# A decoder block on one core: one fill and one LayerNorm schedule moved, the first two FFNs started four slots earlier, and five waits changed

## The reference

```
x = x + selfattn(layernorm(x))        # q, k, v, o projections with biases, causal softmax
x = x + crossattn(layernorm(x), ctx)  # q = layernorm(x), k = v = ctx, causal, no projections
n = layernorm(x)
out = x + relu(n @ W_up.T) @ W_down.T + rw * (n @ W_expert)   # rw: sum of softmax over the top 2
```

## Time and profile before

| what | us |
|---|---|
| median of 3 executions | 713.16 (711.97 to 713.25) |
| the profiled execution | 711.97 |
| its span | 710.0 |
| VectorE busy | 494.6 |
| ScalarE busy | 501.4 |
| GpSimd busy | 256.9 |

### The profile page before, as it was taken

How to read it: one execution, slowest core, us unless ns; L and a number is a source line. 1 busy time by engine, 2 the same in 40 slices (tenths; PEclk the granted TensorE clock), 3 DMA queues, 4 the chain that set the end, 5 groups by cost and what they waited for, 6 DMA issues and landing times.

```text
span 710.0 us, 13884 instructions
## 1 busy us (share of the span) xinstructions
PE 674.7 (95%) x4488; PEld 523.8 (74%) x4488; DVE 494.6 (70%) x1730; ACT 501.4 (71%) x1450; POOL 256.9 (36%) x391
## 2 busy tenths in 40 slices
PE   7998999999999999999889987999989999899998
PEld 6777777777787777777666755777768777677786
DVE  6568766766766776776878788767887669664632
ACT  5678877777876778787899887776588667874110
POOL 4745644333555335742564415333112102000100
PEclk9999999999999999999999999999999999999999
DMA  9763533336423573445946584633463443510101
GB/s 313 186 155 75 141 70 90 82 94 185 116 61 90 124 212 84 102 105 146 275 122 168 153 236 121 166 95 97 96 183 89 111 101 87 163 38 1 59 1 59
DMA packets 52327, 86.12 MB, mean 121 GB/s; under 512 B 8609, under 2 KB 16801, under 8 KB 52257
## 3 DMA queue, kind: packets, MB, share of 16 engines
q1 hardware_dynamic: 52256, 85.25, 46.1%
HBM read 27.55 MB, written 7.34 MB: 49 GB/s over the span
## 4 chain that ended last, share of the span: by engine, by line
PE 80%; DVE 7%; ACT 6%; issue 2%; DMA 2%; POOL 2%; SPq 1%; POOLq 0%; ACTq 0%; DVEq 0%
PE t L480 16%; PE m L519 14%; PE m L520 14%; PE m L521 14%; PE pv L513 9%; PE s L466 8%; DVE probs L682 3%; ACT probs L910 3%; ACT prob L919 1%; PE m L585 1%; DVE prob L692 1%; DMA stack<-stage 1%; POOL probs L1023 1%; PE m L480 1%; PE m L534 1%
## 5 line engine op out<-in xcount | busy, mean ns | idle before, releaser
L682 DVE CUSTOM_DVE_ANT_0 probs<-s,mask 128x128 f32<-128x128 f32 (+3 forms) x512 | 246.6, 483 | 130.7 <-PE s L466 129.0
L910 ACT ACTIVATE probs<-probs,negmax 128x128 f32<-128x128 f32 (+3 forms) x512 | 284.5, 559 | 46.1 <-DVE negmax L682 45.2
L480 PE MATMUL t<-ident,probs 128*128 128x128 f32 x1140 | 203.5, 277 | 11.4 <-ACT prob L919 6.5
L466 PE MATMUL s<-stack 96*128 96x128 f32 (+3 forms) x512 | 197.8, 394 | 5.5 <-DVE negmax L682 2.8
L1023 POOL TENSOR_SCALAR probs<-probs,rsum 128x128 f32<-128x128 f32 (+3 forms) x256 | 133.4, 539 | 176.9 <-DVE rsum L696 176.6
L919 ACT ACTIVATE prob<-t 128x384 f32<-128x384 f32 (+1 forms) x231 | 124.7, 540 | 97.7 <-PE t L480 96.7
L480 PEld LDWEIGHTS t<-ident,probs 128*128 128x128 f32 x1140 | 144.7, 141 | 60.6 <-ACT prob L919 10.5
L466 PEld LDWEIGHTS s<-stack 96*128 96x128 f32 x512 | 97.9, 191 | 18.7 <-DVE negmax L682 4.1
L910 ACT ACTIVATION_READ_ACCUMULATOR probs<-probs,negmax 128x1 f32 x512 | 98.9, 193 | 0.0
L692 DVE COPY prob<-t 128x256 f32<-128x256 f32 (+1 forms) x218 | 77.1, 354 | 30.9 <-PE t L480 29.9
L519 PE MATMUL m<-xT_hi,w_lo 128*128 128x512 f32 x192 | 78.3, 408 | 1.2 <-DVE xT_lo L750 1.2
(11 more groups left out here) (144 smaller groups left out, 946.2 us busy)
## 6 DMA issues: line engine op xcount, KB each, us to landing
stack<-stage SPq DMA_DIRECT2D x384, 128.0 KB, 2.3
xt<-in_x SPq DMA_DIRECT2D x16, 256.0 KB, 4.7
xres<-in_x SPq DMA_DIRECT2D x4, 1024.0 KB, 6.1
kraw<-in_ctxT SPq DMA_DIRECT2D x16, 256.0 KB, 3.0
cv<-in_ctx SPq DMA_DIRECT2D x16, 256.0 KB, 3.1
x<-xres SPq DMA_DIRECT2D x3, 1024.0 KB, 5.5
res<-x SPq DMA_DIRECT2D x8, 256.0 KB, 6.4
out<-res SPq DMA_DIRECT2D x2, 1024.0 KB, 4.8
```

The costliest lines, as they stand in the source:

```text
L466: nc.tensor.matmul(score_tile(P, i), stack[0:RS, P % 2, h, 0, chunk(qb)], stack[0:RS, P % 2, h, 1, 0:N], start=True, stop=True).then_inc(s ...
L480: mm = nc.tensor.transpose(dst[:, chunk(qb - kb)], probs[:, (2 * P + h) % 3, OFF[qb] + PART * kb:OFF[qb] + PART * kb + PART], ident[:, :])
L682: nc.vector.tensor_tensor_reduce(probs[:, (2 * P + h) % 3, OFF[qb]:OFF[qb + 1]], score_tile(P, i), mask[:, T - N:T], -SCALE, BIG, ALU.add, ...
L910: nc.scalar.activation(tile, tile, ACT.Exp, bias=negmax[:, P % 2, h, qb:qb + 1], scale=-1.0, accum_out=total).then_inc(p_exp, 1)
```

## The change

- FEED: the FFNs start at slots 340, 404, 472 and 536; the first two 4 slots sooner. The gap of 4 slots without fills after the second becomes one of 8.
- stats_slots: norm 5 has its four statistics in slots 272, 272, 273, 273 instead of 256, 256, 272, 272; norm 6 in 344, 345, 348, 349 instead of 339 to 342 (with that, ln_scale(6) goes from step 42 to step 43).
- plan: L(b,3) one slot sooner (slot 0 of its step, not 1), O(b,3) of batches 0 and 1 too; FL at distances 1, 3, 5, 7 instead of 1, 2, 4, 5.
- turn: in cross attention, one wait for all four exponentials of the head stands ahead of the first transposes, instead of one wait ahead of each.
- FG: part c multiplies lo and hi of chunk c, instead of hi of all chunks in parts 0 and 1 and lo in 2 and 3.
- GpSimd no longer waits for VectorE's norms 5 to 7 and the four FFN norms ahead of the key split.

```diff
--- before.py
+++ after.py
@@ -74,7 +74,7 @@
 WARM = 24
 
 
-FEED = tuple(PAIRS * (PAIRS * (f + B + 1) + 2) + PAIRS for f in range(B))
+FEED = tuple(PAIRS * (PAIRS * (f + B + 1) + 2) + 4 + 4 * (f // 2) for f in range(B))
 
 
 def own(G):
@@ -104,8 +104,8 @@
         z -= 2 * PAIRS if j == B else 0
         return [z - 8, z - 7, z, z + 1]
     if j == B + 2:
-        return [z + 19, z + 20, z + 21, z + 22]
-    return [z, z, z + 16, z + 16] if j == B + 1 else [z, z, z + 1, z + 1]
+        return [z + 24, z + 25, z + 28, z + 29]
+    return [z + 16, z + 16, z + 17, z + 17] if j == B + 1 else [z, z, z + 1, z + 1]
 
 
 def norm_slots(j):
@@ -148,7 +148,7 @@
             if b:
                 put(("V", b, t), PAIRS * b - 3 + t, 4, 4)
                 if t:
-                    put(("L", b, t), PAIRS * b - 5, 4 + t + 2 * (t // 3), 1)
+                    put(("L", b, t), PAIRS * b - 5, 4 + t + t // 3, 1)
             else:
                 put(("V", b, t), t - 2, 4, 4)
             if b == B - 1:
@@ -156,13 +156,13 @@
             elif b == B - 2:
                 put(("O", b, t), (25, 28, 29, 29)[t], 4 * (t // 3), 4)
             else:
-                put(("O", b, t), PAIRS * (b + 1) + 1 + t, (4, 4, 0, 1)[t], 4)
+                put(("O", b, t), PAIRS * (b + 1) + 1 + t, 4 if t < 2 else 0, 4)
     for f in range(B):
         u = feed_start(f)
         put(("FG", f), 0, u + GATE_AT, 4, 3)
         for m in range(KC):
             if f < B - 1:
-                put(("FL", f, m), 0, u + 1 + m + m // 2, 1, 1)
+                put(("FL", f, m), 0, u + 1 + 2 * m, 1, 1)
             put(("FU", f, m), 0, u + UP_AT + 4 * m, 4)
             put(("FE", f, m), 0, u + EXP_AT + 4 * m, 4)
             put(("FD", f, m), 0, u + DOWN_AT + 4 * m, 4)
@@ -469,14 +469,14 @@
             def turn(P, i):
 
                 h, kb = divmod(i, NT)
+                if kb == 0 and not own(P // 2):
+                    pe.wait_ge(p_exp, PAIRS * P + NT * (h + 1))
                 if TURN_BEFORE[P, i] is not None:
                     pe.wait_ge(*emptied(TURN_BEFORE[P, i]))
                 dst = turned_tile(P, i)
                 for qb in range(kb, NT):
                     if kb == 0 and own(P // 2):
                         pe.wait_ge(p_done, PAIRS * own_rank(P) + NT * h + qb + 1)
-                    elif kb == 0:
-                        pe.wait_ge(p_exp, PAIRS * P + NT * h + qb + 1)
                     mm = nc.tensor.transpose(dst[:, chunk(qb - kb)],
                                              probs[:, (2 * P + h) % 3, OFF[qb] + PART * kb:OFF[qb] + PART * kb + PART],
                                              ident[:, :])
@@ -577,13 +577,11 @@
                         pe.wait_ge(f_ln, NT * (n + 1))
                     turn_x(dst, f_xln, m).then_inc(fl_mm, 1)
                 elif kind == "FG":
+                    pe.wait_ge(fl_lo, KC * n + c + 1)
                     if n == 0 and c == 0:
                         pe.wait_ge(g_lo_done, 1)
-                    done, x_part = (fl_hi, xT_hi) if c < KC // 2 else (fl_lo, xT_lo)
-                    for k in (2 * c % KC, 2 * c % KC + 1):
-                        pe.wait_ge(done, KC * n + k + 1)
-                        mm = nc.tensor.matmul(dst, g_both[:, k, :], x_part[:, k, :], start=(c == 0 and k == 0),
-                                              stop=(c == KC - 1 and k == KC - 1))
+                    nc.tensor.matmul(dst, g_both[:, c, :], xT_lo[:, c, :], start=(c == 0), stop=False)
+                    mm = nc.tensor.matmul(dst, g_both[:, c, :], xT_hi[:, c, :], start=False, stop=(c == KC - 1))
                     if c == KC - 1:
                         mm.then_inc(gate_mm, 1)
                 elif kind == "FU":
@@ -1107,12 +1105,6 @@
                 if own(s // 2):
                     for qb in range(NT):
                         scaled(s, 1, qb)
-                for j in range(B + 1, 2 * B):
-                    if s == norm_slots(j)[-1] // PAIRS:
-                        pool.wait_ge(ln_done, NT * (j + 1))
-                for f in range(B):
-                    if s == f_norm_slots(f)[-1] // PAIRS:
-                        pool.wait_ge(f_ln, NT * (f + 1))
                 if s % 2 == 0 and other(s // 2 + 2):
                     keys(s // 2 + 2)
                 if own((s + 1) // 2):
```

## The result

| | before | after |
|---|---|---|
| median (range, executions) | 712.70 (711.97 to 713.25, 4) | 722.98 (721.55 to 724.09, 4) |
| the profiled execution | 711.97 | 721.66 |
| its span | 710.0 | 719.6 |
| mean granted clock | 0.995 | 0.990 |

The changed kernel is slower: ratio 1.0144, interval 1.0119 to 1.0168. The forecast was 715.0, its range ended at 717.9. A second measurement of the same changed kernel, among the experiments, gave 1.0086 (1.0066 to 1.0106). Both lie on the slower side, and neither is as small as the forecast's 1.0027 (1.9 of 712). So the direction was right and the size was not.

What follows compares the result with a forecast made beforehand. TensorE, busy 674.7 of 710 us, was taken as the bound, with VectorE or ScalarE bounding stretches around the FFNs. Terms summed to +1.9 on 711.97, giving 713.9, stated as a median of 715.0; range 711.5 to 717.9.

Steps and rivals of the forecast that it cites:

- point 1: L3 and O3 moved to slot 0 make TensorE wait ahead of the values: +4.0 us over three batches.
- 4: First FFN's earlier start and norm 6's moved statistics use VectorE's idle time in slots 336 to 351: -1.9 us.
- point 6: Gap after the second FFN, 12 to 16 slots without matmul parts, slots 464 to 484: -1.3 us.
- 3: Without GpSimd's waits the key split runs beside step 42's four FFN norms: +0.9 us on VectorE, counted in 4.
- point 5: Gap after the first FFN, now slots 400 to 411, priced by ScalarE's work, and the gate's turn leaving later: -0.6 us.
- point 2: Norm 5's statistics leave slot 256, two stand in 273, and GpSimd's next scaling starts later: +0.2 us.
- 4, step 44: In step 44 the gate's 8 matmuls are replaced by 12 of FU, less a wait that goes: +0.7 us.
- the hole: A 0.5 us hole in ScalarE's work in the present gap, added once for both FFN gaps: +0.5 us.
- 7: Last FFN's new gate order leaves one more matmul after the last xT_lo, +0.2 us; merged exponentials wait, +0.1.
- rival C: Clearly slower: opening gains nothing and low clock enters the 16 slots without matmuls; +5.5 us, 718.7, chance 0.08.

Runs made afterwards that it cites:

- e11_after_stats: Changed kernel with the statistics of norms 5 and 6 back in their old slots: 723.46 us, 1.0120 against the kernel before.
- a2_after: Changed kernel run again unchanged, the table's second profile of after: 719.80 us, 1.0086 against the kernel before.
- e2_wait: Kernel before without GpSimd's waits for VectorE's norms, nothing else changed: 714.86 us, 0.9994.
- e8b_after_wait: Changed kernel with GpSimd's waits for the norms put back, timed in a later job beside the changed kernel: 718.19 us, 1.0072 against the kernel before.
- e1_lo: Kernel before with only L(b,3) and O(b,3) moved one slot sooner: 719.89 us, 1.0081.
- e10_after_fl: Changed kernel with FL back at the old distances 1, 2, 4, 5: 717.17 us, 1.0042 against the kernel before.
- e3: Kernel before with the change's FEED and FL distances, nothing else: 717.40 us, 1.0036.
- e5: Kernel before with the change's FEED alone, FL at its old distances: 715.03 us, 1.0017.
- c1: Kernel before with all four FFNs 4 slots sooner, FL at its old distances: 715.58 us, 1.0019.
- c2_all4_stats: Kernel before with all four FFNs 4 slots sooner and norm 6's statistics in the changed kernel's slots: 711.72 us, 0.9962.
- b2_before: Kernel before run again unchanged, the table's second profile of before: 714.13 us, span 711.9.
- e4_gate_turn: Kernel before with the new order of FG and the merged wait for the exponentials: 713.35 us, 0.9989.
- e8: Changed kernel with GpSimd's waits for the norms put back, first timing: 718.72 us, 1.0062 against the kernel before.
- e9: Changed kernel with L(b,3) and O(b,3) back in their old slots: 714.94 us, 1.0020 against the kernel before.

## Why the prediction was wrong

The sum was +1.9 and the profiled executions differ by 9.6; without the start, the second pair of profiles differs by 6.9. The sign held because point 1 held, the one large loss that I had. The size failed because the gains of points 4 and 6 didn't come: I forecast -1.9 and -1.3, and they measured -0.6 and +0.9. Of the 5.0 us between 1.9 and 6.9, point 6 is 2.2, points 3 and 4 are 1.3, point 1 is 0.8 and point 5 is 0.7. The terms, in the order of the prediction:

| point | predicted | after against before | after, again against before, again |
|---|---|---|---|
| 1, L3 and O3 | +4.0 | +4.7 | +4.8 |
| 2, norm 5 | +0.2 | +0.3 | +0.3 |
| 3 and 4, slots 328 to 352 | -1.9 | +1.1 | -0.6 |
| 4, step 44 | +0.7 | +0.7 | +0.7 |
| 5, first gap, with the hole's +0.5 | -0.1 | +0.6 | +0.6 |
| 6, second gap | -1.3 | +0.9 | +0.9 |
| 7, tail and merged wait | +0.3 | +0.25 | +0.25 |
| the start | 0 | +1.1 | -0.9 |

**1 was right in its mechanism, and in size for two of three batches.** O3 waited 0.72 and L3 0.44 where I said 0.8 and 0.7, the steps of b = 2 and 3 grew by 1.67 and 1.64 (predicted 1.65). For b = 1 I had 0.7 and the step grew by 1.37. Slot 32 is 1.38 longer (L3's wait of 0.86 and its 0.6) and slot 33 0.44 shorter, as worked, but then slots 34 to 36 are 0.41 longer: there I had taken 0.2 off for a wait that would shorten, and instead the turn of a tile into an m bank came to wait for the evacuation of L3:

```profile
76.17 0.33 PE L480 MATMUL m<-ident,probs 128*128 128x128 f32 x1 [0.55 <-DVE xT_lo L766]
```

That the turns use the m banks too was in the description of the kernel, and I had followed only the fills.

**2 and the step 44 term of 4** came out in size. For point 2, e11_after_stats takes 0.2 of its 0.3 back, and kernels with the old plan of this place differ among themselves by 0.1 (87.24 to 87.35).

**3 failed in its price.** I read 0.79 for a norm beside a GpSimd operation as the price of any overlap, 0.25 each. That norm had only the end of the other engine's operation before it, and even so it waited for that end. This is the subtraction beside it, in the profile of before:

```profile
285.44 1.29 POOL L1058 TENSOR_TENSOR stage<-kraw,stage 128x512 fp32r<-128x512 f32 x1
```

It ends at 286.73 and the norm of the earlier trace rows at 287.02, 0.29 later. The rows after show the same with more left to wait: the first subtraction ends at 435.68 and the pair of norms at 435.97. In the profiles of all runs there are 103 of these 128x512 operations that took longer than 0.57 us, and each of them ended 0.28 to 0.29 us after the end of a GpSimd operation, however long that still had to run. So the price of an overlap is the time that GpSimd's operation has left, less about 0.26 (an estimate: 0.54 alone less 0.28), and not a fixed 0.25. The two pairs took 2.01 and 1.98 us instead of 1.00 and 0.91, so +2.1 and not +0.9. a2_after has 2.01 and 1.78, e2_wait 2.02 for its first pair. The Trainium skill ("SBUF — State Buffer", Who interferes with whom) calls the shared port pair an exclusive lock, and I wrote that the trace did not agree. Read to the end, both traces agree with it. By the rule I had 2.7 for the four norms, by my reading at most 1.0; 2.1 came. I also gave the key splits beside the norms of the later FFNs nothing. In step 50 of the changed kernel, VectorE and GpSimd:

```profile
520.84 1.28 POOL L1056 TENSOR_TENSOR stage<-kraw,stage 128x512 fp32r<-128x512 f32 x1
```
```profile
521.07 1.79 DVE L743 TENSOR_SCALAR f_xln<-res,f_mv,f_rstd 128x512 f32<-128x512 f32 x2
```

That pair takes 1.00 in e8b_after_wait. It is 0.5 of point 5 (400 to 424 at 29.93 there against 30.45).

**4 failed on the basis of comparison and on the first part of the gate.** "I give 2.8 of it back", the idle time of VectorE. Against a profile of before that has the usual low stretch, 0.6 came back (from slot 336 on 0.5, and 0.2 against e1_lo with 22.56). The runs name three things. The norms took 1.2 more than I gave them (2.1 instead of 0.9), and the waits put back recover 0.5 of the stretch from 336 on. The distances of FL cost 1.1 (e10_after_fl 28.90 against 30.00), and from 336 on 2.0 (20.30 against 22.32): the third part one slot later and the fourth two let the gate's first part wait 2.18 for an xT_lo, which is 0.44 in e10, and e10 has one low stretch here where a2_after has two. That holds with the statistics moved; with the statistics in their old slots I can't see a cost of the distances here (24.23 in e3, 24.52 and 22.94 in e5 and c1 without them). I wrote that this wait "is inside this", which was an assertion, without a sum behind it. And before's profile was 1.6 below its second one in this stretch, so part of what I subtracted from was luck; the mean clock of 0.92 in the earlier trace rows is one low stretch in 21.5 us where the other profile has two. The statistics are the part that works: -3.7 from c1_all4 to c2_all4_stats and +3.0 in e11_after_stats when taken back. And the early start with them alone does open the stretch as I had thought: c2 takes 19.53 from 336 on, 3.3 less than b2_before. The distances (2.0) and the norms beside GpSimd (0.5) used most of it up.

**5 failed by norms that had no term, not at the gate's turn.** Slots 416 to 419 take 7.41 (predicted 7.4), and 420 to 423 take 0.46 less (predicted 0.45). But slots 400 to 415 take 18.07 where my sum of ScalarE's prices had 16.85, or 17.35 with the hole's 0.5. With GpSimd's waits put back they take 17.55. So 0.5 is the norm pair that I had given nothing, and the sum with its hole was right within 0.2. (The terms that I name for it, 3.08, 7.05 and 6.57, add up to 16.70; the 16.85 has 0.15 more that the text doesn't explain.)

The same 16 slots by stretch, first of the changed kernel with the four slots behind them, then of e8b_after_wait. The new plan's gap answers to the last four stretches of the earlier trace rows:

```profile
518.60:536.70 18.10, 15.07 (x122) 11.65 (x121) 16.39 (x56) 15.09 (x45) 6.27 (x7) 1.00 0.64 176
536.70:544.10 7.40, 7.40 (x63) 5.06 (x62) 4.91 (x19) 4.79 (x15) 0.00 (x0) 1.00 0.61 142
```
```profile
517.50:535.00 17.50, 14.97 (x121) 11.59 (x120) 15.82 (x56) 15.01 (x45) 4.43 (x5) 1.00 0.65 182
```

ScalarE has the same 15.0 to 15.1 us of work in both; VectorE has 0.6 more and GpSimd is busier in the first, and the stretch is 0.5 longer.

**6 failed by the clock.** The 16 slots took 16.08 us to the score of 480, where I said 15.9, and the gate's wait came, 1.57 against 1.5. But the clock fell under the values behind it, 3.72 us instead of 2.36, and slots 464 to 483 took 25.51 instead of 23.25. In e8b_after_wait, where the clock stays, they take 23.88, which the hole's 0.5 covers but for 0.1. A low clock was rival C, at 0.08, and I looked for it inside the 16 slots; it came right behind them. The old distances take wait and low clock away at once, 28.86 and 28.30 for 464 to 488. So the loss of this place comes from the distances of FL and not from the earlier FEED.

**7 was right**: the tail is 0.25 longer, and e4_gate_turn finds nothing for the merged wait and the gate's order. The hole of 0.5 was put in once, and each of the two gaps used it.

**What stays open.** The start (23.9 to 26.7 us in these profiles, no edit touches it) gave the first profile of the changed kernel 1.1 us that are chance. The two timings of the changed kernel, 1.0144 and 1.0086, have four executions each and intervals that don't meet; the profiles' terms speak for the lower one, and I have no run that explains the higher one (its executions had a mean granted clock of 0.988 to 0.990, those of a2_after 0.990 to 0.995). That the wait of 1.57 brings the low clock is an inference: it came in the profiles of after, a2, e3, e8, e9 and e11 and not in e8b, which all have the wait, and never in e5, e10, c1 or c2. No experiment changed the clock alone; e8 and e8b are one kernel, with the same wait, and only one of them has the low clock. Of distances between the transposed parts and the gate only the two of the kernels were tried. L(b,3) and O(b,3), and the gate's order and the merged wait, were only tried together.

## What to carry to other kernels

An instruction moved ahead on an in-order queue costs above all its wait: 0.7 and 0.6 us of matmuls put in front of the values cost 1.65 net, of which 1.16 are their two waits, because the evacuations that they needed were not due yet. Before predicting from one profile, look which stretches carry a low clock and ask whether the next execution would have it in the same place; here that was worth 1.6 us at one place, most of the forecast gain. And where an overlap of VectorE and GpSimd is new, price it by what the other engine's operation has left to run, not by one case that only touches the other's end.

## What the runs showed of the hardware

- A pair of 128x512 scalings on VectorE takes 0.91 to 1.00 us alone and 1.78 to 2.28 under GpSimd's casts and subtractions: both pairs of the first FFN in after, a2, e9 and e10, the first pair in e2 and e11, and the first pair of the second and third FFN (1.78 to 1.80) in all six. By my price of 0.25 a norm it would have been 1.5. A lengthened one ends 0.28 to 0.29 us after the GpSimd operation, in 103 of 103 cases.
- TensorE's 32 value matmuls of step 42 take 2.36 us at 2.4 GHz by the rows of other steps, and 3.6 to 4.5 with most of them at 1.2 GHz. What TensorE did before was 5.35 busy us in 7.90 in the changed kernel. It came in both kernels: in both profiles of the changed one, and in the second of the unchanged one. In the first the values took 2.68 at a granted clock of 1.00.
- A low stretch needn't cost time. The first profile of the unchanged kernel has one from 356.2 to 359.6 us, while ScalarE is busy for every one of its 3.4 us, and the second has none there; slots 240 to 328 take 87.24 and 87.26.
- The wait of slot 336's score for its stack DMA lasted from 0.62 to 4.02 us over 16 profiles.
- Executions of one program, the kernel before, ran from 711.3 to 718.3 us on one chip (26 executions, median 714.11), so 0.2% is only reached with many of them.
